# Preparation of a six-stage transformer kernel moved out of its start, and an output bias added by TensorE instead of GpSimd

## The reference, cut to what matters

```
x = x + 0.5 * moe(norm(x))     # 8 experts, top 2, hidden 128: relu(x w1)^2 w2, gates from the router
x = x + linear_attention(...)  # causal prefix sums per head (16 heads of 8), divided by a denominator
x = x + 0.5 * moe(norm(x))     # the same experts
x = x + 0.5 * fp4_ffn(...)     # gated, hidden 352, operands rounded to FP4 in blocks of 16
x = x + token_attention(...)   # softmax over the 8 batch rows of one position; in and out bias
x = x + 0.5 * fp4_ffn(...)
```

## Time and profile before

| what | value |
|---|---|
| median of 3 runs (range) | 868.86 us (866.7 to 873.04) |
| profiled execution: its own time | 870.8 us |
| its span | 869.0 us |
| TensorE busy, x records | 703.0 us (81%), 6018 |
| VectorE busy | 676.8 us (78%), 1671 |
| ScalarE busy | 466.8 us (54%), 893 |
| GpSimd busy | 164.6 us (19%), 323 |
| mean granted TensorE clock | 0.896 of 2.4 GHz |
| `accumulate` L819, VectorE | 512 at 345 ns, 147.8 us |
| `pv` L998, VectorE | 32, shortest 1209 ns, longest 3381 ns |
| `add_bias` L369, GpSimd | 4, shortest 2342 ns, longest 3327 ns |

### The profile page before, as it was taken

How to read it: one execution, slowest core, us unless ns; L and a number is a source line. 1 busy time by engine, 2 the same in 40 slices (tenths; PEclk the granted TensorE clock), 3 DMA queues, 4 the chain that set the end, 5 groups by cost and what they waited for, 6 DMA issues and landing times.

```text
span 869.0 us, 17382 instructions
## 1 busy us (share of the span) xinstructions
PE 703.0 (81%) x6018; PEld 533.8 (61%) x6018; DVE 676.8 (78%) x1671; ACT 466.8 (54%) x893; POOL 164.6 (19%) x323
## 2 busy tenths in 40 slices
PE   3999999798986999999585777468989865857774
PEld 2777776677775677776354665436686663546654
DVE  2888787375656578789799999649899956999995
ACT  3787777656460677777464455264323114644552
POOL 4001021645542100101111210022110001112100
PEclk9999999899999899999768788868999987687888
DMA  7000000000000000000000000000000000000000
GB/s 197 2 0 0 0 1 2 3 3 2 0 3 3 1 1 0 0 1 0 1 0 0 0 0 0 1 0 1 1 0 0 1 0 1 12 12 12 12 24 25
DMA packets 13454, 6.99 MB, mean 8 GB/s; under 512 B 1177, under 2 KB 13409, under 8 KB 13409
## 3 DMA queue, kind: packets, MB, share of 16 engines
q1 hardware_dynamic: 10464, 5.26, 2.3%
q10 hardware_dynamic: 2944, 1.12, 0.5%
HBM read 4.28 MB, written 2.10 MB: 7 GB/s over the span
## 4 chain that ended last, share of the span: by engine, by line
PE 60%; DVE 26%; issue 7%; ACT 3%; DMA 1%; POOL 1%; DVEq 0%; SPq 0%; POOLq 0%; ACTq 0%
PE ps L1171 53%; PE ps L1470 4%; DVE ffn_work L723 3%; DVE shared L998 2%; DVE ffn_work L728 2%; DVE picked L900 2%; PE ps L1483 2%; DVE hq L734 1%; DVE x_sb L819 1%; DVE xn L734 1%; ACT xn L435 1%; DVE ffn_work L717 1%; DVE fq_x_max L700 1%; DMA wraw<-ttn_out_proj_weight_dram 1%; DVE attT L906 1%
## 5 line engine op out<-in xcount | busy, mean ns | idle before, releaser
L1171 PEld LDWEIGHTS ps<-w_sb,sq_h 128*128 128x128 f32 x1024 | 131.9, 192 | 68.8 <-ACT sq_h L457 50.7
L819 DVE SCALAR_TENSOR_TENSOR x_sb<-ps,gates,x_sb 128x128 f32 (+1 forms) x512 | 147.8, 345 | 20.4 <-PE ps L1171 12.3
L294 POOL TENSOR_SCALAR vareps<-meanvar 128x4 f32<-128x4 f32 (+1 forms) x44 | 25.0, 568 | 606.4 <-DVEq L763 606.4
L1171 PE MATMUL ps<-w_sb,sq_h 128*128 128x128 f32 x1024 | 138.0, 278 | 0.9 <-ACT sq_h L457 0.9
L1171 PE MATMUL ps<-xnT,w_sb 128*128 128x512 f32 x256 | 135.4, 613 | 0.0
L453 ACT ACTIVATE relu_h<-ps 128x512 f32<-128x512 f32 x128 | 75.7, 591 | 57.6 <-PE ps L1171 57.3
L435 ACT ACTIVATE xn<-x_sb,shift,rstd 128x128 f32 (+1 forms) x192 | 79.8, 481 | 18.3 <-POOL shift L302 18.2
L457 ACT ACTIVATE sq_h<-relu_h 128x512 f32<-128x512 f32 x128 | 80.6, 630 | 4.0
L1483 PE MATMUL ps<-ident,xn 128*128 128x128 f32 x64 | 16.8, 414 | 70.8 <-DVE xn L734 70.8
L1171 PE MATMUL ps<-ident,shared 128*128 128x128 f32 x512 | 64.6, 290 | 10.3 <-DVE shared L998 10.3
L1171 PE MATMUL ps<-downT,hqT 128*128 128x128 f32 x384 | 71.2, 339 | 0.5 <-ACT hqT L631 0.5
(11 more groups left out here) (147 smaller groups left out, 1270.1 us busy)
## 6 DMA issues: line engine op xcount, KB each, us to landing
x_sb<-in_L_attn_x_dram SPq DMA_DIRECT2D x8, 256.0 KB, 6.4
out_dram<-x_sb SPq DMA_DIRECT2D x8, 256.0 KB, 2.3
w_sb<-in_L_ffn_w_all_dram ACTq DMA_DIRECT2D x2, 512.0 KB, 7.4
wraw<-in_L_attn_qkv_w_dram SPq DMA_DIRECT2D x1, 192.0 KB
wraw<-attn_in_proj_weight_dram SPq DMA_DIRECT2D x1, 192.0 KB
fraw<-in_L_ffn_w_down_dram SPq DMA_DIRECT2D x1, 176.0 KB, 3.5
fraw<-in_L_ffn_w_gate_dram SPq DMA_DIRECT2D x1, 128.0 KB, 4.0
fraw<-in_L_ffn_w_up_dram SPq DMA_DIRECT2D x1, 128.0 KB, 3.1
```

Of the source, the lines that this page charges most:

```text
L819: t = nc.vector.scalar_tensor_tensor(tile_b(i, j), bank(4 + e % 4, TPB, C)[:, j, :], gates[:, j, e:e + 1], tile_b(i, j), ALU.mult, ALU.add)
L1171: return nc.tensor.matmul(o, a, b, start=start, stop=stop, **kw)
```

## The change

The seven other rows of x are loaded before the attention weights, and the six small parameter loads move from ScalarE's queue to the end of these on SyncE's. At the start TensorE turns only the router weights. The eight attention blocks are turned in the last group of the first experts (four after e = 1, four after e = 3) and copied out by ScalarE at e = 2 and e = 4. Abs, Exp and Ln move behind ScalarE's loop, between groups 5 and 6. The denominator (VectorE) moves into the last group: its base after e = 0, its reciprocal in four quarters after e = 1 to 4. GpSimd builds the tie-break table first. The output bias is no longer added by GpSimd: TensorE writes it into the two output banks, as a product of the identity with the broadcast bias, ahead of the contexts, and `project_out` accumulates onto it.

```diff
@@ SyncE queue @@
-            sp_q.dma_start(rraw[:, :], router_w).then_inc(s_w, 16)
+            sp_q.dma_start(rraw[:, :], router_w).then_inc(s_r, 16)
+            for b in range(1, B):
+                sp_q.dma_start(x_sb[:, TPB * b:TPB * b + TPB, :],
+                               x[b, :, :].rearrange("(c p) f -> p c f", p=P)).then_inc(s_x1 if b == 1 else s_x, 16)
             ... (the four wraw loads, unchanged)
-            for b in range(1, B):
-                sp_q.dma_start(x_sb[:, TPB * b:TPB * b + TPB, :], ...).then_inc(s_x, 16)
+            ... (the two head_par, three in_b_col and one out_b_all loads, moved here from the ScalarE queue)
@@ GpSimd @@
             pool.sem_inc(s_ident, 1)
+            one(nc.gpsimd.memset(tiebreak[:, :, :], -0.5))
+            one(nc.gpsimd.affine_select(out=tiebreak[:, :, :], ...))
+            pool.sem_inc(s_tie, 1)
             ...
                 elif ph == "att":
-                    def add_bias(i):
-
-                        pool.wait_ge(s["xn_ready"], i + 1)
-                        nc.gpsimd.tensor_tensor(slots_t(i, 0, B), slots_t(i, 0, B),
-                                                out_b_all[:, :].unsqueeze(1).to_broadcast([P, B, C]),
-                                                ALU.add).then_inc(s["bias_added"], 1)
-
-                    pool.wait_ge(s_par, 64)
                     ln_group(s, 0, B)
                     ln_group(s, 1, B)
                     with pool.Fori(0, TPB - 2) as i:
-                        add_bias(i)
                         ln_group(s, i + 2, B)
-                    add_bias(TPB - 2)
-                    add_bias(TPB - 1)
@@ ScalarE @@
-            ... (the six small loads; Abs, Exp and Ln of the head parameters ahead of everything)
             act.dma_start(w1_sb[:, :, :], w1.rearrange("e c f -> c e f")).then_inc(s_w1, 16)
             act.dma_start(w2_sb[:, :, :], w2.rearrange("e f c -> f e c")).then_inc(s_w2, 16)
+            def softplus_terms():
+                act.wait_ge(s_head, 32)
+                nc.scalar.activation(sp[:, 0, :], head_par[:, :], ACT.Abs).then_inc(s_sp, 1)
+                act.wait_ge(s_sp, 1)
+                nc.scalar.activation(sp[:, 1, :], sp[:, 0, :], ACT.Exp, scale=-1.0).then_inc(s_sp, 1)
+                act.wait_ge(s_sp, 2)
+                nc.scalar.activation(sp[:, 2, :], sp[:, 1, :], ACT.Ln, bias=1.0).then_inc(s_sp, 1)
+            act.wait_ge(s_rT_done, 1)
+            nc.scalar.activation(rT[:, :], bank(1, E), ACT.Copy).then_inc(s_rT, 1)
+            def attention_weights_out(part):
+                act.wait_ge(s_wT_done, part + 1)
+                ... (the same copies to wT as before: one for part 0, two for part 1, out of bank 1)
@@ ScalarE, moe @@
                         if e == 6 and not more and first:
                             evac_xnT(nxt, 0)
+                        if first and not more and e in (2, 4):
+                            attention_weights_out(e // 2 - 1)
             ...
                     body(i, True, 0)
                     body(i + 1, True, 1)
+                if first:
+                    softplus_terms()
                 body(GROUPS - 2, True, 0)
                 body(GROUPS - 1, False, 1)
@@ VectorE @@
-            dve.wait_ge(s_head, 32)
-            prep.add(nc.vector.tensor_scalar(sp[:, 3, :], head_par[:, :], 0.0, None, ALU.max))
-            def inverse_denominator():
-                dve.wait_ge(s_prep_act, 3)
+            def denominator_base():
+                dve.wait_ge(s_const, 1)
+                dve.wait_ge(s_head, 32)
+                prep.link(nc.vector.tensor_scalar(sp[:, 3, :], head_par[:, :], 0.0, None, ALU.max))
+                dve.wait_ge(s_sp, 3)
                 ... (the five linked operations up to pos, unchanged)
-                prep.link(nc.vector.reciprocal(pos[:, :], pos[:, :]))
+            def inverse_part(k):
+                prep.add(nc.vector.reciprocal(pos[:, P * k:P * k + P], pos[:, P * k:P * k + P]))
@@ VectorE, moe body, after the accumulates of expert e @@
+                        if first and not more and e == 0:
+                            denominator_base()
+                        if first and not more and e in (1, 2, 3, 4):
+                            inverse_part(e - 1)
@@ VectorE, moe start @@
-                    dve.wait_ge(s_x, 16 * (B - 1))
+                    dve.wait_ge(s_x1, 16)
                     dve.wait_ge(s["xn_ready"], 1)
                     ln_stats(s, ch, 1, TPB, tile_b)
-                    dve.wait_ge(s_const, 1)
-                    inverse_denominator()
+                    dve.wait_ge(s_tie, 1)
                 gating(0, lambda j: None)
+                if first:
+                    dve.wait_ge(s_x, 16 * (B - 2))
@@ VectorE: linatt queries(0) first waits for the reciprocals; att residual(i, k) @@
-                    dve.wait_ge(s["bias_added"], i + 1)
@@ TensorE @@
             pe.wait_ge(s_ident, 1)
-            pe.wait_ge(s_w, 80)
-            ... (transposes of rraw and of the eight blocks of wraw; waits for s_w12 and for the copies)
+            pe.wait_ge(s_r, 16)
+            nc.tensor.transpose(bank(1, E), rraw[:, :], ident[0:E, 0:E]).then_inc(s_rT_done, 1)
+            def attention_weights_turned(part):
+                if part == 0:
+                    pe.wait_ge(s_w, 64)
+                    pe.wait_ge(S["moe_a"]["sub_ready"], GROUPS)
+                else:
+                    pe.wait_ge(s_wT, 1)
+                for k in range(4):
+                    t = nc.tensor.transpose(bank(1, 4, P)[:, k, :], wraw[:, 4 * part + k, :], ident[:, :])
+                t.then_inc(s_wT_done, 1)
@@ TensorE, moe body, after down(i, e) @@
+                        if first and not more and e in (1, 3):
+                            attention_weights_turned(e // 2)
@@ TensorE, moe start @@
+                if first:
+                    pe.wait_ge(s_rT, 1)
                 router(0, 0)
+                if first:
+                    pe.wait_ge(s_w1, 16)
+                    pe.wait_ge(s_w2, 16)
                 up(0, 0, 0)
@@ TensorE: linatt waits for s_wT (2) before project_in(0); att @@
+                def bias_out(i, more):
+
+                    pe.wait_ge(s["xnT_ready"], 2 * i + (4 if more else 2))
+                    if not more:
+                        pe.wait_ge(s["out_free"], 2 * i + 2)
+                    for k in range(2):
+                        mm(bank(k, 4, C), ident[:, :], out_b_all[:, :].unsqueeze(1).to_broadcast([P, 4, C]),
+                           start=True, stop=False, skip_group_check=True)
+
                 def project_out(i, k):
                     pe.wait_ge(s["ctxT_ready"], 2 * i + k + 1)
                     for j in range(4):
-                        t = mm(bank(k, 4, C)[:, j, :], turned[:, 4 * k + j, :], woT)
+                        t = mm(bank(k, 4, C)[:, j, :], turned[:, 4 * k + j, :], woT, start=False, stop=j == 3,
+                               skip_group_check=True)
             ...
                     if more:
                         make_qk(i + 1)
+                    bias_out(i, more)
                     for b in range(B):
                         context(i, b)
```

More of the change, by code:

```diff
@@ L259, in _ @@
             sp_q.dma_start(wraw[:, 7, :], out_w).then_inc(s_w, 16)
-            for b in range(1, B):
-                sp_q.dma_start(x_sb[:, TPB * b:TPB * b + TPB, :],
-                               x[b, :, :].rearrange("(c p) f -> p c f", p=P)).then_inc(s_x, 16)
+            sp_q.dma_start(head_par[:, 0:1], alpha_log.rearrange("(h a) -> h a", a=1).to_broadcast([H, HD])
+                           .rearrange("h (d a) -> h d a", a=1)).then_inc(s_head, 16)
+            sp_q.dma_start(head_par[:, 1:2], beta_log.rearrange("(h a) -> h a", a=1).to_broadcast([H, HD])
+                           .rearrange("h (d a) -> h d a", a=1)).then_inc(s_head, 16)
+            for a in range(3):
+                sp_q.dma_start(in_b_col[:, a:a + 1], in_b.rearrange("(h a d o) -> h a d o", a=3, d=HD, o=1)[:, a, :, :]
+                               ).then_inc(s_par, 16)
+            sp_q.dma_start(out_b_all[:, :], out_b.rearrange("(a f) -> a f", a=1).to_broadcast([P, C])).then_inc(s_par, 16)
             sp_q.wait_ge(s_fraw0, 1)
@@ L288, in _ @@
             pool.sem_inc(s_ident, 1)
+            one(nc.gpsimd.memset(tiebreak[:, :, :], -0.5))
+            one(nc.gpsimd.affine_select(out=tiebreak[:, :, :], in_=tiebreak[:, :, :], compare_op=ALU.is_ge, fill=0.5,
+                                    base=0, pattern=[[-1, E], [1, E]], channel_multiplier=0))
+            pool.sem_inc(s_tie, 1)
             nc.gpsimd.memset(fraw[:, :], 0.0).then_inc(s_fraw0, 1)
@@ L310, in _ @@
             one(nc.gpsimd.memset(headsel[:, :], 1.0))
-            one(nc.gpsimd.memset(tiebreak[:, :, :], -0.5))
             one(nc.gpsimd.memset(headcols[:, :], 0.0))
@@ L315, in _ @@
                            allow_small_or_imprecise_dtypes=True))
```

(34 more changed lines are left out.)

36 lines of the change are left out of this document (13 added, 23 removed).

## The result

The changed kernel takes 863.56 us (median of 9 runs, 860.53 to 865.45) beside 870.42 us (864.45 to 873.04, 9 runs) for the kernel before: ratio 0.9929, 95% interval 0.9904 to 0.9955. The forecast was 863.0. Its profiled execution took 863.56 itself, 7.2 less than that of before; the sum had said 5.9 less.

What follows compares the result with a forecast made beforehand. Bounds: attention-weight landing and ScalarE at the start, then TensorE, VectorE at the linear-attention seam. Terms -6.6 + 1.3 + 5.2 + 1.0 - 6.8 = -5.9 took 868.9 to 863.0 us, range 857.5 to 868.5.

Steps and rivals of the forecast that it cites:

- The start: First group: with the attention weights out of the way, the router starts at 11.5 instead of 18.07, 6.6 us earlier.
- the head wait: Start: VectorE's sums began at 6.73, behind an operation waiting for head parameters until 6.61; that wait is removed too.
- Softplus: Between groups 5 and 6: Abs, Exp, Ln and two table loads on ScalarE partly exceed its idle time, +1.3 us.
- The denominator: Last group of the first experts: base 1.5 and reciprocal 3.7 lengthen VectorE's gapless run, the chain, by 5.2 us.
- The clock at the seam: Start of the linear attention: TensorE idles 5 us longer, so scores start at the lower clock, +1.0 us.
- The bias: Token attention: faster pv and shorter waits give -2.0, avoided clock falls in three passes -4.8, together -6.8 us.
- The slower one: Rival, 6%: slow pv isn't GpSimd's doing, so the token attention gives +1.3 in place of -6.8; 871.1 us.
- The hidden addition: Rival, 9%: scores wait for something other than VectorE, so the seam costs 0 instead of 6.2; 856.8 us.
- The start gains less: Rival, 12%: router weights hold ScalarE or w2 holds TensorE, start gains about 3.5 in place of 6.6; 866.1 us.
- The clock falls all the same: Rival, 15%: the clock still falls in the token attention, so its 4.8 us are not gained; 867.8 us.

Runs made afterwards that it cites:

- e9: Changed kernel plus, in each pass, a GpSimd zero fill of a 128x1024 array nothing else uses, in the old addition's place: 863.78 us, ratio 0.9944.
- e8: Changed kernel with the attention weights loaded ahead of the x rows, turned and copied at the start again: 866.85 us, ratio 0.9954.
- e6: Changed kernel with head parameters first on ScalarE's queue and VectorE waiting for them ahead of its first sums, as before: 864.87 us, ratio 0.9937.
- e3: Changed kernel with Abs, Exp and Ln moved into ScalarE's idle time at the start, behind the first xnT copy: 862.07 us, ratio 0.9907.
- e4: Changed kernel with Abs, Exp, Ln moved to the start and the denominator behind the first gating's comparisons: 858.42 us, ratio 0.9878.
- e1: Kernel before with only the bias half of the change, identity products in place of the GpSimd addition: 864.26 us, ratio 0.9933.
- e5: Changed kernel plus a GpSimd addition of the old size and place in each pass, between arrays nothing else touches: 867.65 us, ratio 0.9966.
- e2: Kernel before with the two identity products a pass added, without effect on the result, the GpSimd addition staying: 867.99 us, ratio 0.9978.
- e10: Changed kernel without any output bias, neither products nor addition, its waits kept: 859.98 us, ratio 0.9899.
- e7: Changed kernel with early softplus and denominator, plus 28 identity transposes on TensorE ahead of the first group: 857.84 us, ratio 0.9852.

## Why the prediction was right, step by step

**The start, -6.6.** The mechanism and the place are right: x lands at 4.30 (said: 4.3), sums 4.33, router 11.57 (said: 11.5). What failed is the tacit step that the 6.5 reach the end of the group. TensorE ran 7.7 us at half rate behind the router, 5.0 before, and 5.26 arrived. I had read the clock only where it fell, not where the start's half rate ends; in e9, with the same start, that came at about 16.5, and at router 7 the start's gain is 128.48 - 123.08 + 1.14 (the softplus) = 6.5. Of the causes that I named, e8 and e6 give the turning 3.8 at the router and the head wait 1.65; that the weights landed late because of the parameter loads I had not seen.

**Softplus, +1.3.** Measured 1.14 (router 7 gained 4.12 where the second group had gained 5.26), and 1.13 by e3. The price that I had cited, about 2.7 us per switch (the Trainium skill, "ScalarE: Activation LUTs", section "Table sets: the hidden batching unit"), is not what this trace shows: the load is 1.28 and the next activation starts 0.01 behind it.

**The denominator, +5.2.** Group 7 grew by 3.81, so 1.4 less, the largest miss in the sum. The base ran for 1.5 as said, the reciprocals for 0.94 each. The failed step is that they add their full length between the accumulates. The sets of four accumulates came 1.23 apart; with a reciprocal between them they come 1.81 apart, 0.6 more and not 0.9. The 0.2 us that VectorE had let pass between two sets, and another 0.1 at the first of a set, now lie under the reciprocal, and the base adds 1.3 in the same way. In all this makes 3.6; the last 0.2 appears ahead of it, between two small operations of the gating, and stays unexplained. I costed the turning at nothing, or at 1.2 if it were not covered. That holds: e8, which has it at the start, has the same 23.58, and e4, without cover, shows 0.96.

**The clock at the seam, +1.0.** The clock is at half before the scores begin, as expected, but the chain's piece from the scores on is 8.49 long against 8.12: 0.4. Timeline after, TensorE:

```profile
154.79 3.52 PE L1185 MATMUL ps<-shared,phi_k 32*32 32x128 f32 x128 [1.62 <-issue]
...
161.81 1.47 PE L1185 MATMUL ps<-wT,xnT 128*128 128x128 f32 x8
```

The scores took 0.7 more (2.81 before), and the eight products 0.3 less (1.81 before), because the full rate came back sooner behind the scores' start. I had priced the earlier fall and not the earlier return. Over the whole middle even the 0.4 is gone (421.43 against 421.45).

**The bias, -6.8.** Measured -6.49, in e1 as well. By passes, from the starts of the scores: -3.4 (said -2.7), -3.9 (-3.8), +0.8 (+1.3), 0 (-1.6). Pass 0: the two waits cost 3.4 and not 3.0, since the records ahead of each ran out into it for another 0.2; the products cost 1.7 and not 1.9; the slow records gave 1.7, near the 1.6. Pass 3 was wrong in kind: its contexts are fast now, but the second block waits 1.62 for VectorE, whose `pv` is the chain there and had hidden the slow contexts before. Two misses that cancel.

**The rivals.** The slower one (the slow `pv` isn't GpSimd's doing) is refuted by e1, e5 and e9. The hidden addition is refuted by e4, which gained 2.85 in group 7 by removing it. "The start gains less" did not come as described: the router products, at 11.57, waited for ScalarE's copy of `xnT` alone, and `up` behind them did not wait for `w1` or `w2`. Less arrived for the clock's reason. "The clock falls all the same" did not happen: the contexts are fast in the changed kernel and in all ten of the experiments, but my reason for it, shorter waits, is not the cause shown: e2 keeps the 2.27, e10 has 2.58. What decides whether it falls stays open. The Trainium skill, "TensorE: Matmul & The Clock Gate", Part 1, holds that the moment at which the chip looks is not tied to the kernel, so that one kernel shows different transitions; the two rises from one code (19.3 and 16.5 us) agree, and no run here moves the same waits in time alone to test it on the falls.

**The total.** The steps said -5.9. The trace has -5.26 + 1.14 + 3.81 = -0.31 up to `phi_k`, nothing in the middle, -6.49, and -0.3 in the last stage, together -7.2. The sum was near because the start, put 1.3 too good, stood against the denominator (1.4 too dear) and the seam (1.0 too dear): misses that cancel, which is luck. So is part of the hit on the time. The 868.9 that the sum was taken from is the median of three runs; over nine it is 870.4, and from there the same sum gives 864.5. The medians moved by 6.9.

## What to carry to other kernels

Before moving work out of the start, look who idles in the start: here ScalarE and VectorE had gaps of several us there, and work moved into group 7 went onto VectorE's chain for 2.85 us that the gaps would have taken free. Take two-input additions on GpSimd away from two-input instructions of VectorE that others wait for; two products a pass with the identity, into banks that are accumulated anyway, cost 1.2 us where the addition cost 5.5 (e5 against after), or 7.7 with the slow contexts (before against e10). And read a gain at a clock boundary only behind it: what arrives is what the next group shows, not what the router shows.

## What the runs showed of the hardware

- At the start the granted clock reads 1.00 while products take their half-rate times (0.94 per 512 columns, 0.51 later), up to 16.5 or 19.3 us; it reads 0.50 there only in e7, where TensorE had run at full rate before. Durations, not the clock column, tell the rate there.
- In e7 transposes of the identity brought TensorE to full rate during the loads; idle stretches of 1.56 and 0.56 us later it fell to 0.50, and stayed there from 10.8 to 17.6 us although its rows show it busy.
- A wait of 2.3 to 2.6 us ahead of the contexts went with half clock in the kernel before and with full clock in e2, e5 and e10.
- The last stage, whose code is the same everywhere, takes 145.7 to 146.0 us or 143.8 to 143.9 us. The short one came in e2, e5 and e10 alone, with the higher clock. All runs of these three show a mean clock of 0.907 to 0.919, and those of the other changed kernels, but for one far outside, 0.895 to 0.903, so it is not the chance of one execution. It gave back 1.8 of e5's 5.5 us; why is open.
- While two loads of 0.5 KB stood first on one queue (before, e6), the DMA engines moved 58 and 61 GB/s from 3 to 4 us; with these loads later (after, e8) they moved 302 and 318.
